# Two attention products change places between two PSUM banks, and the low halves of the first norm are made in steps 0 and 1 instead of 2 and 4

## What is computed

```python
h = jnp.maximum(_layernorm(x, axis=-1), 0.0)
x = x + _L0_gnn_ref(h, adj, Wq, bq, Wk, bk, Wv, bv, Wo, bo)      # 16 heads, softmax over the masked scores, then @ Wo
h = jnp.maximum(_layernorm(x, axis=-1), 0.0)
x = x + _L1_gnn_ref(h, adj, weight, wq, wk)                      # alpha = relu(q k^T) * mask, softmax(axis=1), alpha^T (h @ weight)
```

## Time and profile of the kernel before

| | |
|---|---|
| median of three runs | 1640.91 us |
| the profiled execution | 1642.58 us, of which the span is 1640.8 us |
| PE busy | 1509.1 us, 92% |
| DVE busy | 1294.3 us, 79% |
| ACT busy | 1129.7 us, 69% |
| POOL busy | 1005.8 us, 61% |
| DMA | 226.27 MB, mean 138 GB/s |
| chain that ended last | PE 48%, DVE 33%, issue 10%, ACT 4% |

### The profile page before, as it was taken

How to read it: one execution, slowest core, us unless ns; L and a number is a source line. 1 busy time by engine, 2 the same in 40 slices (tenths; PEclk the granted TensorE clock), 3 DMA queues, 4 the chain that set the end, 5 groups by cost and what they waited for, 6 DMA issues and landing times.

```text
span 1640.8 us, 50717 instructions
## 1 busy us (share of the span) xinstructions
PE 1509.1 (92%) x16561; PEld 1107.6 (68%) x16561; DVE 1294.3 (79%) x4202; ACT 1129.7 (69%) x2477; POOL 1005.8 (61%) x1286
## 2 busy tenths in 40 slices
PE   2879999999999999999999999999999999999996
PEld 1547777767777676777767676777667777767763
DVE  5778888787888887788888888888878888887763
ACT  2567767777776777777777777677777767777661
POOL 1546666666666666666666666666666666666551
PEclk9989999999999999999999999999999999999998
DMA  8647766666667656656665666666566666666760
GB/s 230 126 78 142 129 153 149 145 134 135 140 134 159 148 133 148 134 130 145 153 149 126 152 137 127 152 151 145 128 145 142 128 153 148 145 135 135 131 116 26
DMA packets 656198, 226.27 MB, mean 138 GB/s; under 512 B 611489, under 2 KB 627873, under 8 KB 656161
## 3 DMA queue, kind: packets, MB, share of 16 engines
q1 hardware_dynamic: 636848, 188.57, 55.6%
q10 hardware_dynamic: 19312, 37.23, 7.4%
HBM read 57.94 MB, written 16.78 MB: 46 GB/s over the span
## 4 chain that ended last, share of the span: by engine, by line
PE 48%; DVE 33%; issue 10%; ACT 4%; POOL 1%; DMA 1%; DVEq 1%; ACTq 1%; SPq 0%; POOLq 0%
PE ring L407 38%; DVE wk_raw L847 7%; DVE stage L928 3%; PE score L459 3%; PE pv L478 3%; DVE half L907 3%; DVE x L949 2%; ACT stage L652 2%; DVE newton L890 2%; DVE stage L925 2%; DVE stats L866 1%; DVE o_sum L862 1%; PE ring L513 1%; DVE work L967 1%; DVE l_max L982 1%
## 5 line engine op out<-in xcount | busy, mean ns | idle before, releaser
L1104 POOL TENSOR_TENSOR wv_raw<-wk_raw,wv_raw 128x512 f16<-128x512 f32 x512 | 609.3, 1192 | 482.6 <-ACT wv_raw L630 482.4
L617 ACT ACTIVATE wk_raw<-wk_raw,least 128x256 f32<-128x256 f32 x1024 | 458.8, 497 | 11.8 <-DVE least L847 11.8
L847 DVE CUSTOM_DVE_ANT_0 wk_raw<-score,far,undo_score 128x256 f32<-128x256 f32 x1024 | 441.8, 478 | 11.7 <-DVE far L1018 11.4
L630 ACT ACTIVATE wv_raw<-wk_raw 128x512 f16<-128x512 f32 x512 | 320.3, 626 | 9.7 <-issue 5.5
L478 PE MATMUL pv<-val,turned 128*128 128x65 f16 x2048 | 185.5, 192 | 12.5 <-DVE o_sum L862 7.3
L478 PEld LDWEIGHTS pv<-val,turned 128*128 128x128 f16 x2048 | 150.5, 97 | 61.2 <-issue 35.8
L407 PE MATMUL ring<-wv_hi,h 128*128 128x256 f16 x1024 | 189.3, 273 | 0.0
L407 PE MATMUL ring<-h,wq_hi 128*128 128x256 f16 x1024 | 176.7, 274 | 7.6 <-DVE wk_lo L810 7.6
L480 PE MATMUL pv<-val,turned 128*128 128x33 f16 x2048 | 177.9, 179 | 0.0
L407 PE MATMUL ring<-h,wk_hi 128*128 128x256 f16 x1024 | 176.5, 274 | 0.0
L1123 POOL TENSOR_TENSOR heads_out<-o_sum,o_rcp 128x64 f32<-128x64 f32 x512 | 140.7, 295 | 51.3 <-DVE o_sum L862 47.5
(11 more groups left out here) (147 smaller groups left out, 3586.6 us busy)
## 6 DMA issues: line engine op xcount, KB each, us to landing
xin<-x_dram ACTq DMA_DIRECT2D x32, 512.0 KB, 3.7
out_dram<-xo SPq DMA_DIRECT2D x32, 512.0 KB, 3.5
xa<-x_dram ACTq DMA_DIRECT2D x31, 512.0 KB, 4.0
adj_in<-adj_dram SPq DMA_DIRECT2D x32, 256.0 KB, 2.8
turned<-wv_raw SPq DMA_TRANSPOSE x512, 3.1
adjt_in<-adj_t_dram SPq DMA_DIRECT2D x32, 256.0 KB, 3.1
wq_raw<-wq_dram SPq DMA_DIRECT2D x2, 512.0 KB, 6.3
wk_raw<-wk_dram SPq DMA_DIRECT2D x2, 512.0 KB, 8.0
```

The source lines that it names most:

```text
L617: last = nc.scalar.activation(probs[:, at, q, :], probs[:, at, q, :], ACT.Exp, bias=least[:, at, q:q + 1], scale=-1.0)
L630: nc.scalar.activation(halves[:, at, :, 0, :], probs[:, at, :, :], ACT.Copy).then_inc(hi["p"], 1)
L847: last = nc.vector.tensor_tensor_reduce(out=probs[:, at, q, :], in0=score[u % GROUP][:, q * NODES:(q + 1) * NODES], in1=far[:, q, :], scal ...
L1104: nc.gpsimd.tensor_tensor(halves[:, at, :, 1, :], probs[:, at, :, :], halves[:, at, :, 0, :], ALU.subtract).then_inc(lo["p"], 1)
```

## The change

It edits two constants. In `BANK` the entries of `av0` and `av1`, the two halves (by nodes) of the second attention's product, are exchanged. By `bank_before` this alters four waits of PE in the body of graph t:

| product, step | bank and the low half it waits for, before | after |
|---|---|---|
| `av0`, 14 | bank 2: `qk1` of graph n, made in step 13 | bank 0: `hw1` of graph p, made in step 12 |
| `av1`, 15 | bank 0: `hw1` of graph p, step 12 | bank 2: `qk1` of graph n, step 13 |
| `qk2a`, 0 | bank 0: `av1`, step 15 of the body before | bank 0: `av0`, step 14 of the body before |
| `ot1`, 1 | bank 2: `av0`, step 14 of the body before | bank 2: `av1`, step 15 of the body before |

In the first body `av0`'s place is taken by the search for a scale of the merged weights, which moves from bank 2 to bank 0 with it. `LOW1_STEPS` goes from (2, 4) to (0, 1), so that DVE makes the two low halves of the first norm behind the masks of step 0 and of step 1. They are the same two instructions for each graph, and DVE makes them ahead of the low halves of `ot1` and `qk2` in step 1 instead of ahead of those of `wo0` (step 2) and `qk3` (step 4). No instruction is added or taken away.

```diff
@@ -64,8 +64,8 @@
 BANK = {"qk2": 0, "wo0": 1, "ot1": 2, "wo1": 2, "qk3": 0, "v1": 1, "h2_0": 2, "h2_1": 0, "g0": 2,
-        "g1": 0, "hw0": 1, "qk0": 2, "al": 0, "ot0": 1, "qk1": 2, "hw1": 0, "v0": 1, "av0": 2,
-        "av1": 0}
+        "g1": 0, "hw0": 1, "qk0": 2, "al": 0, "ot0": 1, "qk1": 2, "hw1": 0, "v0": 1, "av0": 0,
+        "av1": 2}
@@ -81,7 +81,7 @@
-HIGH1_STEP, LOW1_STEPS, TURN1_STEP = 14, (2, 4), 6
+HIGH1_STEP, LOW1_STEPS, TURN1_STEP = 14, (0, 1), 6
```

## The result

The changed kernel takes 1626.97 us (median of four runs, 1625.34 to 1628.41) beside 1641.89 us for the kernel before: a ratio of 0.9903, with a 95% interval from 0.9891 to 0.9915. It is faster, as forecast, but by 15 us and not by 56: it lies above the whole range on record. Its profiled execution took 1625.34 us, of which the span is 1623.6 us.

What follows compares the result with a forecast made beforehand. PE was taken as the bound, with DVE idle 9.1 us a pass. The terms 1.63 - 0.10 + 0.84 - 0.03 - 0.46 = 1.88 us, times 30, gave 56 us and a forecast of 1584.5 us; whole range 1568 to 1600.

Steps and rivals of the forecast that it cites:

- PE is the bound: In the loop PE limits; its waits before `av0` and `h2_1` lose 1.63 and 0.82 to 0.87 us a pass.
- The banks: Steps 14 and 15: `av0`'s 1.63 us go, 0.10 is paid at `av1`, and PE from `av1` on runs 1.53 us earlier.
- What is late next is `av1`: Behind `av0`, `av1` is due at 829.86 and finds the low half of `qk1` at 829.96: 0.10 us paid.
- The low halves in steps 0 and 1: Two low halves at 0.69 us each make `ot1`'s low half, and so `wo0b`, 0.46 us late (0.30 to 0.62).
- Rival 3: A moved low half waits for one POOL instruction, delaying `ot1`'s low half and `wo0b`: 35 us, 1619; chance 5%.
- `h2_1` gets its 0.84 us: Step 5: freeing steps 2 and 4 of low halves removes 0.84 us of `h2_1`'s wait, with 0.03 left.
- The sum: All terms for each of 30 passes: 1.88 us (1.59 to 2.10), together 56 us (48 to 63).
- Rivals 1 and 2: 1: DVE from step 5 to 13 keeps its own pace, 1595, 9%; 2: turned heads land late, 1599, 8%.
- Rival 5: Something else holds `av0`, so only step 5 gains: 10 us, 1630; chance 4%.

Runs made afterwards that it cites:

- e1_banks: Only the exchange of the `av0` and `av1` banks, low halves left in steps 2 and 4, against the kernel before: 1616.43 us, ratio 0.9837.
- e6: Changed kernel with the second low half in step 2, and step 13's second mask moved behind the head pair's sum in step 14: 1587.51 us.
- e9: As e6, but low halves in step 15 of the body before and step 0, and the sum ahead of `qk1`'s low half: 1573.97 us.
- e10: As e1_banks, but DVE's sum of the head pair ahead of the low half of `qk1` in step 13: 1607.96 us, ratio 0.9788.
- e4: POOL's x1 addition (L1148) made in eight instructions instead of two, against the changed kernel: 1604.99 us, ratio 0.9773.
- e5: POOL's L1148 replaced by a one-input copy without the bias, against the changed kernel: 1611.3 us, run once.

## Why the prediction was wrong, point by point

- **PE is the bound, and its two waits are worth 1.63 and 0.82 to 0.87 us a pass.** Right: 1.64 us, and 0.84 at `h2_1` (0.87 before, 0.03 after). The rest of a pass stayed at 45.4 to 45.5 us in all runs.
- **The banks: "What is late next is `av1`".** This is the step that failed first. Between `av0` and `av1` PE weighs head 14, and I looked only at the semaphores of the banks. With `av0` at once, that weighing is due 1.29 us after 828.33, at about 829.6, and the sum that it needs ended only at 829.91 + 0.39 = 830.30. With the 0.05 us from there to the weighing that is 0.7 us late, which could have been read from the kernel before; it measured 0.75. This wait hides the 0.10 us of `av1`. So the exchange is worth 1.64 - 0.75 = 0.89 us a pass, not 1.53. e1_banks shows it; e6, e9 and e10 show that it is the sum. The row of the sum in the timeline of before:

```profile
829.91 0.39 DVE L862 TENSOR_REDUCE o_sum<-pv 128x128 f32<-128x256 f32 x1
```

- **The low halves in steps 0 and 1 make `wo0b` 0.46 us later.** The mechanism is right, the size wrong: 1.22 - 0.14 = 1.08 us. Without the hold-up by POOL (e4) it is 0.41 - 0.14 = 0.27 us, less than I said; the held-up low half adds 0.81. The term that failed is the duration of one low half, 0.61 to 0.77 us in my bounds and 1.50 in step 1.
- **Rival 3, DVE locked out by POOL, at 5%.** It is what happened, at 22 us (e4 against the changed kernel) and not the 35 of its price. I held it down with one pair of rows, the low half at 849.27 that ran in 0.68 us while POOL was inside L1157. That pair did run so, in all 30 passes, and stays unexplained; but the instructions that the moved halves would really meet, L1123 in step 0 and L1148 in step 1, I did not look at. The kernel before already had such a meeting, in step 2. The low half at 842.83 starts 0.07 us after the L1123 shown below, and ends at 843.60, 0.55 us after it. That is the 0.77 against 0.68 which I put beside L1104. L1104 started only at 843.01 and was itself the one held up (1.61 us). The Trainium skill (SBUF — State Buffer, section Who interferes with whom) names just this pairing, two SBUF inputs on DVE and a read on POOL, and the runs agree with it: 1.50 us with 0.96 us of POOL's instruction still to run, 0.98 us with 0.44. The pair with L1157 does not.

```profile
842.76 0.29 POOL L1123 TENSOR_TENSOR heads_out<-o_sum,o_rcp 128x64 f32<-128x64 f32 x1
```

- **`h2_1` gets its 0.84 us.** Right: 0.87 - 0.03 = 0.84. The next product, `g0`, took 0.15 back, a term that the sum did not have.
- **The sum.** On record 1.63 - 0.10 + 0.84 - 0.03 - 0.46 = 1.88 us a pass. Measured 1.64 - 0.75 + 0.84 - 1.08 - 0.15 = 0.50, and the pass is 0.50 us shorter: 30 times that is 15 us, which is the result. Of the 1.38 us that are missing, the banks make 0.64 and `wo0b` 0.62.
- **Rivals 1 and 2.** DVE's work in steps 5 to 13 did follow PE: the low half of `qk1` starts 2.41 us behind the first matmul of `v0a` both before (829.43 after 827.02) and after (870.84 after 868.43). PE waited for a head's transpose 4 times in the whole changed kernel, 3.8 us in all, and 5 times before.
- **Rival 5.** Its figure, 1630, lies 3 us from the result, and that is chance: it has nothing won at the banks and 0.35 us by the low halves, where the banks won 0.89 and the low halves lost 0.39.

## What to carry to other kernels

Where a wait is taken away, go through every instruction of that queue up to the next thing that is known to be late, and for each through all of its semaphores, not only those of the resource that the change touches; the trace of before has the times of all of them. Where an instruction is moved, look up what the other engines do at its new place: its duration at the old place is no bound if the two engines hold each other up, and if the other side comes first, what is left of its one instruction is the price. Idle time ahead of an instruction that waits for another engine is the cheap place, and it holds only as much as it is long.

## What the runs showed of the hardware that was not expected

In these runs a DVE instruction with two SBUF inputs (L907) that started while POOL was inside an instruction on SBUF was held until about the end of it, with one exception. It took 1.50 us instead of 0.68, ending 0.54 us after POOL's, against a two-input addition of 1.27 us, and 0.98 us, again ending 0.54 us after POOL's, against a one-input copy of 0.62 us. Cut into pieces of 0.46 us, the same addition held it by nothing that can be seen (0.69 us): 0.15 us of the first piece were left, and it ended 0.54 us after that piece, too. An instruction with one PSUM and one SBUF input (L941) was not held, with 1.2 us of POOL's addition still to run.

It works the other way as well: whichever came second was held. The second half of the addition, behind the low half, took 1.72 us in place of 1.27, and a POOL instruction of 0.29 us (L1123), met by the first low half in step 0, took 0.74. In all these pairs the later one ended its own undisturbed time, less about 0.14 us, after the end of the earlier one (0.68 - 0.54; 1.27 - 1.13, from 881.06 to 882.19).

The exception is L1157, which reads one int32 tensor: the low half that started with 0.47 us of it left took its 0.68 us in all 30 passes. Why stays open; no run was made for it, and the copy in e5, which also has one input (f32), did hold the low half.
